# One tile a round by one-row DMAs of SyncE and ScalarE in place of a gather of GpSimd

## The reference, cut to what matters

```python
# layer 0: attention over the edges of each dst node
h = x @ W
e = leaky_relu((h @ att_src)[src] + (h @ att_dst)[dst], 0.2)     # self loops added
e = exp(e - segment_max(e, dst)[dst])
x = layernorm(x + tanh(segment_sum(h[src] * (e / denom[dst])[:, None], dst) + bias))
# layer 1: messages
h = gelu(x @ W_pre + b_pre)
x1 = x + segment_sum(h[src] * edge_attr, dst)
x = layernorm(x + x1 + gelu(gelu(x1 @ W1 + b1) @ W2 + b2))
```

## Time and profile before

| | |
|---|---|
| median of 3 runs | 3743.58 us |
| the profiled execution, its whole time | 3744.99 us |
| its span | 3743.2 us |
| GpSimd busy | 2782.9 us (74%), 2950 instructions |
| VectorE busy | 2422.9 us (65%) |
| TensorE busy | 2393.7 us (64%) |
| ScalarE busy | 1303.4 us (35%) |
| mean busy share of the 16 DMA engines | about two tenths in layer 0, four in layer 1 |

### The profile page before, as it was taken

How to read it: one execution, slowest core, us unless ns; L and a number is a source line. 1 busy time by engine, 2 the same in 40 slices (tenths; PEclk the granted TensorE clock), 3 DMA queues, 4 the chain that set the end, 5 groups by cost and what they waited for, 6 DMA issues and landing times.

```text
span 3743.2 us, 65890 instructions
## 1 busy us (share of the span) xinstructions
PE 2393.7 (64%) x16704; PEld 1950.4 (52%) x16705; DVE 2422.9 (65%) x6240; ACT 1303.4 (35%) x3893; POOL 2782.9 (74%) x2950
## 2 busy tenths in 40 slices
PE   5443344344344444444445899999888898999988
PEld 3333333333333333333334777777777777777776
DVE  7444444444566666665656777777777778888886
ACT  5433344444455555555553111111111221111222
POOL 7777777777777777777774777777777777777776
PEclk7555555555555555555556999999999999999998
DMA  5222222222222222222223444444444344444442
GB/s 100 43 41 42 42 44 42 44 42 43 42 43 43 43 44 44 43 43 45 43 43 92 90 93 94 90 95 95 95 94 95 91 95 92 95 95 99 92 95 70
DMA packets 336783, 254.19 MB, mean 68 GB/s; under 512 B 239277, under 2 KB 264370, under 8 KB 336539
## 3 DMA queue, kind: packets, MB, share of 16 engines
q0 software_dynamic: 94016, 146.16, 19.4%
q1 hardware_dynamic: 227905, 99.65, 11.4%
q10 hardware_dynamic: 14618, 6.14, 0.6%
HBM read 244.43 MB, written 7.25 MB: 67 GB/s over the span
## 4 chain that ended last, share of the span: by engine, by line
POOL 42%; issue 22%; PE 12%; DVE 9%; ACT 8%; ACTq 2%; DMA 2%; DVEq 2%; POOLq 0%; SPq 0%
POOL rows L714 42%; PE bank L1161 7%; ACT other L812 4%; PE bank L1148 2%; DVE other L1409 2%; DMA rows<-table,src_i 2%; DVE attr L1412 1%; PE bank L1067 1%; DVE attr L1442 1%; ACTq L803 1%; ACT L855 1%; DVE hot L1613 1%; ACT far_dst L808 0%; ACTq L840 0%; DVEq L425 0%
## 5 line engine op out<-in xcount | busy, mean ns | idle before, releaser
L714 POOL DMA_INDIRECT rows<-table,src_i x2850 | 2695.5, 946 | 912.7 <-issue 851.3
L1161 PE MATMUL bank<-node,hot 128*128 128x288 bf16 x9310 | 1228.8, 294 | 27.7 <-issue 14.7
L1161 PEld LDWEIGHTS bank<-node,hot 128*128 128x128 bf16 x9310 | 931.8, 101 | 282.8 <-issue 17.7
L1613 DVE TENSOR_SCALAR hot<-node,key 128x642 bf16<-128x642 int16 x1862 | 870.2, 538 | 120.1 <-PE bank L1161 64.5
L1063 PE MATMUL bank<-top_diag,ones 40*128 40x40 f32 (+1 forms) x392 | 132.2, 438 | 869.8 <-DVE top_diag L1395 864.7
L1067 PE MATMUL bank<-onehot,rows 128*97 128x72 f32 (+1 forms) x3048 | 543.9, 368 | 85.8 <-issue 85.3
L1063 PEld LDWEIGHTS bank<-top_diag,ones 40*128 40x128 f32 (+1 forms) x392 | 97.8, 309 | 931.7 <-DVE top_diag L1395 926.3
L1067 PEld LDWEIGHTS bank<-onehot,rows 128*97 128x97 f32 x3048 | 512.0, 282 | 118.1 <-issue 117.5
L968 ACT ACTIVATE pair<-dst_i 128x8 f32 (+1 forms) x196 | 35.2, 180 | 1186.2 <-DVE rows L1639 928.9
L812 ACT ACTIVATE other<-iota,far_dst 128x72 f32 (+1 forms) x1564 | 384.3, 328 | 23.1 <-ACT far_dst L808 0.9
L1148 PE MATMUL bank<-onehot,rows 128*96 128x40 f32 (+1 forms) x3128 | 308.1, 256 | 87.9 <-DVE rows L1644 46.3
(11 more groups left out here) (204 smaller groups left out, 1857.2 us busy)
## 6 DMA issues: line engine op xcount, KB each, us to landing
attr<-in_edge_attr_dram SPq DMA_DIRECT2D x190, 336.0 KB
rows<-table,src_i POOLq DMA_INDIRECT x2850
node<-in_src_dram SPq DMA_DIRECT2D x39, 320.0 KB
attr<-in_edge_attr_dram SPq DMA_DIRECT2D x190, 48.0 KB
table<-x SPq DMA_DIRECT2D x12, 196.0 KB
node<-table SPq DMA_DIRECT2D x8, 288.0 KB, 5.1
table<-rowt ACTq DMA_DIRECT2D x15, 144.0 KB
out_dram<-rowt ACTq DMA_DIRECT2D x15, 144.0 KB
```

Of the source, the lines that this page charges most:

```text
L714: pool.indirect_dma_start(to, None, table, bass.IndirectOffsetOnAxis(ap=at, axis=0)).then_inc(landed, 16)
L1161: last = pe.matmul(p_got[t], hot[:, c % HOTS, i, t * P:(t + 1) * P], tab[:, a, :, :].rearrange("p k d -> p (k d)"), start=a == 0, stop=a = ...
L1613: last = v.tensor_scalar(hot[:, c % HOTS, i, :].rearrange("p (r e) -> p r e", r=3), src16[:, :, 0:ROW3], key[:, a:a + 1], None, ALU.is_equal)
```

## The change

In every round but the first, the eighth gathered tile (in layer 1 the seventh) of the fifth group, slot 4, is no longer gathered. Its 128 rows are fetched one by one: 128 plain DMAs of one row each, whose source address comes from a register. In layer 0 SyncE issues 100 of them and ScalarE 28, in layer 1 SyncE 70 and ScalarE 58. They land in one buffer `single` [128 x 98]. In layer 0 ScalarE copies them from there into the slot and the score to PSUM (`given`); in layer 1 VectorE multiplies straight out of `single` (`multiplied_row`). `single` is refilled after it was read.

The addresses, row number times bytes of a row, are made at the start: two loads collect the src numbers of these tiles for all rounds (39 x 128 numbers each, 4 bytes apart from each other in DRAM), ScalarE scales them and stores them to `row_at` in DRAM. Each round both engines load their part of a line of `row_at`, and ten numbers at a time into registers.

Where the rows are issued: in layer 0 SyncE issues 60 once `single` was read (third group of the round before), then waits for the end of that round, loads dst and src as before, and issues 40. ScalarE issues 10 in the fifth group, 10 and 8 in the first two groups of the next round, each time between L839 and `given`. In layer 1 SyncE issues 14 after each attribute load from the fourth slot on, ScalarE 15, 15, 15 and 13 after the feeds in groups 1 to 4.

```diff
+AT_ONCE = 10
+BY_SYNC0, AHEAD0 = 100, 60
+BY_SYNC1 = 70
...
+        def rowed(it, u):
+            return u == SLOTS - 1 and not first(it) and it is not ROUNDS
+
+        def row_bytes(eng, reg, table, n):
+            at = eng.snap(reg, True, min_val=0, max_val=(N - 1) * n * 4)
+            return table.rearrange("n d -> (n d)").bitcast(BYTE)[bass.ds(at, n * 4)].rearrange("(a b) -> a b", a=1)
+
+        def fetch_rows(eng, name, numbers, regs_at, table, n, first_row, landed):
+            for a in range(*regs_at, AT_ONCE):
+                b = min(a + AT_ONCE, regs_at[1])
+                regs = [eng.alloc_register(f"{name}{k}") for k in range(a, b)]
+                eng.load(regs, numbers[0:1, a:b])
+                for k, reg in enumerate(regs, a):
+                    eng.dma_start(row_place(first_row + k, n), row_bytes(eng, reg, table, n)).then_inc(landed, 16)
...
+            last_group = src[0:ROUNDS * SLOTS * GE].rearrange("(r e) -> r e", r=ROUNDS)[:, (SLOTS - 1) * GE:SLOTS * GE]
+            sp.dma_start(made_at[:, 0:P].rearrange("r (p j) -> r p j", j=1),
+                         last_group[:, 0:P * (TILES - 1)].rearrange("r (p j) -> r p j", j=TILES - 1)[:, :, TILES - 2:TILES - 1],
+                         allow_slow_non_contiguous=True).then_inc(s_last, 16)
...
+            def rows_begun0(it, name):
+                sp.wait_ge(sync_at_in, SYNC_AT0 + 16 * it)
+                sp.sem_inc(sync_go, 1)
+                sp.wait_ge(single_free, SINGLE0 + it - 1)
+                sp.sem_inc(sync_go, 1)
+                fetch_rows(sp, f"row0_{name}_", sync_at, (0, AHEAD0), table0, D2, 0, sync_row)
...
                 round_of(dst_i, dst, it, 1 - k, e0.dst[0], 1)
                 if not first(it):
                     round_of(src_i, src, it, 1 - k, e0.src[0], 1)
+                    rows_ended0(it)
+                else:
+                    sp.wait_ge(a_st, 16 * CHUNKS)
+                    sp.wait_ge(act_at_in, 32)
+                row_numbers0(it + 1)
+                rows_begun0(it + 1, it)
...
             def load1(it, k):
                 for u in range(SLOTS):
                     load_attr(it * SLOTS + u, it, u)
+                    load_rows1(it, u)
...
-                    for j in range(TILES):
+                    for j in range(TILES - rowed(it, u)):
                         row_gather(place0(u, it)[:, j * D2:(j + 1) * D2], table0, src_i[:, k, u, j:j + 1], e0.rows[u])
...
-                    for j in range(TILES - booked(it, u)):
+                    for j in range(TILES - booked(it, u) - rowed(it, u)):
...
-                    act.wait_ge(e0.rows[u], gathered(g, it))
-                act.activation(p_src, rows0(u, it)[:, :, D1], ACT.Copy).then_inc(t0.given, 1)
+                    act.wait_ge(e0.rows[u], gathered(g, it, u))
+                t = TILES - rowed(it, u)
+                if rowed(it, u):
+                    act.wait_ge(sync_row, SYNC_ROW0 + 16 * BY_SYNC0 * it)
+                    act.wait_ge(act_row, ACT_ROW0 + 16 * (P - BY_SYNC0) * it)
+                    act.activation(rows0(u, it)[:, t, :], single[:, :], ACT.Copy)
+                    act.activation(p_src[:, t:TILES], single[:, D1:D2], ACT.Copy).then_inc(single_free, 1)
+                act.activation(p_src[:, 0:t], rows0(u, it)[:, 0:t, D1], ACT.Copy).then_inc(t0.given, 1)
...
                         act.activation(onehot_x[:, 0:TILES * w], further_score[:, 0:TILES * w], ACT.Exp).then_inc(tx.w, 1)
+                rows_along0(it, u)
                 if later(g, it, u, 2):
                     given(*later(g, it, u, 2), ws[2])
...
+                if rowed(it, SLOTS - 1):
+                    if u == 0:
+                        load_row_numbers1(it)
+                    if u < SLOTS - 1:
+                        fetch_rows1(it, u)
+
+            BY_ACT1 = (0, 15, 30, 45, P - BY_SYNC1)
...
+            def multiplied_row(it, u):
+                v.wait_ge(sync_row, SYNC_ROW1 + 16 * BY_SYNC1 * it)
+                v.wait_ge(act_row, ACT_ROW1 + 16 * (P - BY_SYNC1) * it)
+                at = slice((TILES - 2) * D, (TILES - 1) * D)
+                v.tensor_tensor(rows[:, u, at], single[:, 0:D], p_attr[:, at], ALU.mult).then_inc(single_free, 1)
```

More of the change, by code:

```diff
@@ L26 @@
 BF16 = mybir.dt.bfloat16
+BYTE = mybir.dt.uint8
 ALU = mybir.AluOpType
@@ L188, in gnn @@
         win_tab = sb("win_tab", [1, 3, GROUPS + 1], INT32)
+        single = sb("single", [P, D2])
+        sync_at = upto[:, 0:P].bitcast(INT32)
+        act_at = run[:, 0:P].bitcast(INT32)
+        made_at = rowt[0:ROUNDS, 0, 0:2 * P].bitcast(INT32)
         group_no = sb("group_no", [TG, 2], INT32)
@@ L330, in gnn @@
         e1_fed = sem("e1_fed")
+        sync_row, act_row, single_free = s_w0, s_dsts, s_tab0
+        sync_at_in, act_at_in = s_x[0], s_x[len(parts) - 1]
+        sync_go, act_go = s_line, s_begun
+        FETCH_ROUNDS = ROUNDS - 1
+        SYNC_ROW0, ACT_ROW0, SINGLE0, SYNC_AT0, ACT_AT0 = 16 * 3, 16 * 6, 1, 16, 32
+        SYNC_ROW1 = SYNC_ROW0 + 16 * BY_SYNC0 * FETCH_ROUNDS
+        ACT_ROW1 = ACT_ROW0 + 16 * (P - BY_SYNC0) * FETCH_ROUNDS
+        SINGLE1 = SINGLE0 + FETCH_ROUNDS
+        SYNC_AT1, ACT_AT1 = SYNC_AT0 + 16 * FETCH_ROUNDS, ACT_AT0 + 16 * FETCH_ROUNDS
         p_top, p_topb, p_newp = bank[0][0:WIN, 0:P], bank[1][:, 0:WIN], bank[1][:, P:P + WIN]
@@ L660, in load_table, with fetch_rows1, load_rows1 @@
                     sp.dma_start(h32[0:N - FULL * P, FULL, :], table1[FULL * P:N, :]).then_inc(landed, 16)
+            SHARE1 = -(-BY_SYNC1 // SLOTS)
+            PORTION1 = [(k * SHARE1, min((k + 1) * SHARE1, BY_SYNC1)) for k in range(SLOTS)]
+            AHEAD1 = 3
+            def fetch_rows1(it, portion, name):
+                if portion == 0:
+                    sp.wait_ge(sync_at_in, SYNC_AT1 + 16 * it)
+                    sp.sem_inc(sync_go, 1)
+                    sp.wait_ge(single_free, SINGLE1 + it - 1)
+                    sp.sem_inc(sync_go, 1)
+                fetch_rows(sp, f"row1_{name}_", sync_at, PORTION1[portion], table1, D, 0, sync_row)
+            def load_rows1(it, u):
+                if first(it):
+                    return
+                if u < AHEAD1 and not second(it):
+                    fetch_rows1(it - 1, SLOTS - AHEAD1 + u, it)
+                if u == AHEAD1 - 1:
+                    sp.dma_start(sync_at[:, 0:BY_SYNC1], row_at[bass.ds(it, 1), 0:BY_SYNC1]).then_inc(sync_at_in, 16)
+                if u >= AHEAD1:
+                    fetch_rows1(it, u - AHEAD1, it)
             def load1(it, k):
@@ L687, in _ @@
             rounds(sp, load1, alone=2)
+            for k in range(AHEAD1):
+                fetch_rows1(ROUNDS - 1, SLOTS - AHEAD1 + k, "last")
             sp.wait_ge(e1.free, LAST + 1)
@@ L823, in given, with load_row_numbers0, fetch_rows0, rows_along0 @@
                 else:
-                    act.wait_ge(e0.rows[u], gathered(g, it))
-                act.activation(p_src, rows0(u, it)[:, :, D1], ACT.Copy).then_inc(t0.given, 1)
+                    act.wait_ge(e0.rows[u], gathered(g, it, u))
[6 more added lines that the diff above has]
+                act.activation(p_src[:, 0:t], rows0(u, it)[:, 0:t, D1], ACT.Copy).then_inc(t0.given, 1)
+            def load_row_numbers0(it):
+                act.dma_start(act_at[:, 0:P - BY_SYNC0], row_at[bass.ds(it, 1), P + BY_SYNC0:2 * P]).then_inc(act_at_in, 16)
+            BY_ACT0 = (0, 10, 20, P - BY_SYNC0)
+            def fetch_rows0(it, part, name):
+                if part == 0:
+                    act.wait_ge(act_at_in, ACT_AT0 + 16 * it)
+                    act.sem_inc(act_go, 1)
+                    act.wait_ge(single_free, SINGLE0 + it - 1)
+                    act.sem_inc(act_go, 1)
+                fetch_rows(act, f"row0_{part}_{name}_", act_at, BY_ACT0[part:part + 2], table0, D2, BY_SYNC0, act_row)
+            def rows_along0(it, u):
+                if it is ROUNDS:
+                    return
+                if True:
+                    if u == SLOTS - 2 and it is not ROUNDS - 1:
+                        load_row_numbers0(it + 1)
+                    if u == SLOTS - 1 and it is not ROUNDS - 1:
+                        fetch_rows0(it + 1, 0, it)
+                    if u < 2 and not first(it):
+                        fetch_rows0(it, u + 1, it)
+                else:
+                    if u == SLOTS - 2 and it is not ROUNDS - 1:
+                        load_row_numbers0(it + 1)
+                    if u < 3 and not first(it):
+                        fetch_rows0(it, u, it)
             def sloped(g, it, u, w):
```

41 lines of the change are left out of this document (36 added, 5 removed).

## The result

The changed kernel takes 4615.19 us (median of 4 runs, 4614.89 to 4618.25) against 3743.53 us for the kernel before on the same chip (3743.04 to 3744.62): a ratio of 1.233, 95% interval 1.231 to 1.235. The profiled execution spans 4613.4 us. The direction was right, the size was not: 3970 us was forecast, 4300 us was the top of the range.

A forecast was written before the change was run, and what follows sets the result against it. Back-to-back gathers were taken as the bound, with ScalarE's serial cycle (layer 0) and VectorE (layer 1) close behind in wide stages; 3745 + 216 + 14 + 4 - 24 + 13 = 3968, say 3970 us, range 3830 to 4300.

The forecast's parts named there:

- What a one-row DMA costs its issuer: Row issue on SyncE and ScalarE: 0.40 us a row, between 0.33 and 0.70, with 0.03 for the register load.
- rival 3: Both layers: rows over 0.46 us make SyncE bound layer 0's narrow rounds; 4298 us at 0.50; chance 0.15 for 4250 or more.
- Layer 0, ScalarE: Rows lengthen its serial cycle: +216 us in wide stage (72 nodes, rounds 19 to 38), +14 in narrow (40 nodes).
- Layer 0, SyncE: SyncE's 100 rows and loads take 46 us, under a round's 48.7; costed at nothing, bound from 0.46 us a row.
- The start: Before layer 0's first group: two loads of single numbers, mostly covered by present waiting, cost 4 us, bounds 0 and 25.
- Layer 1: Rows reach the fifth group's multiply 2 us late: +13 us wide stage, -24 us narrow stage, -11 us together.
- The rule on issuing: Skill's rule for DMA issue: sequencer time is usually small, so ScalarE's rows weigh little; prediction objected that issue is paid per row.
- Rival 1: Both layers: ScalarE's rows fall in time it waits anyway, gathers stay the bound, 3650 us; chance 0.13.
- (1): Layer 0, wide stage: L825 no longer waits for gathered rows; GpSimd waits for L1067 some 10 us a round.
- (2): ScalarE between L839 and L820: gaps of 4 us in three groups of each round, filled with row DMAs.
- (3): Layer 0 rounds, by SyncE's src loads: near 60 us wide and 50 to 51 us narrow.
- (4): Layer 1 rounds: 42.4 us early and 44 to 45 us late, with VectorE waiting for `single`.

The follow-up runs named there:

- moved_b: Changed kernel with row DMAs in layer 0 only, ScalarE's ten rows moved behind the two score copies and ahead of the slope: 3999.9 us.
- act_none: Changed kernel without ScalarE's rows and its waits, SyncE issuing its 100 and 70 as before: 4252.3 us.
- l1_only: Changed kernel with row DMAs in layer 1 only, layer 0 gathering 40 tiles a round, addresses still collected at the start: 4189.5 us.
- fixed_rows: Changed kernel with constant row addresses and no load of registers, so wrong rows are fetched: 4070.3 us.
- the tile for nothing: Changed kernel with each row DMA replaced by a semaphore increment; no row DMAs or register loads left in the trace: 3728.3 us.
- alternate_both_b: Changed kernel with rows in both layers only every second round, all by SyncE, up to twenty registers a load: 3888.11 us, ratio 1.0385.

## Why the prediction was right or wrong

The direction, the reading of both layers' bounds and the mechanism of layer 0 held. The 645 us between 3970 and 4615 us are three terms: layer 0's wide stage 275 for 216, its narrow stage with the start 152 for 18, layer 1 443 for -11.

- **What a one-row DMA costs its issuer: the step that failed first.** The sum took 0.40 us, and 0.50 us was measured. The DMA itself was cheaper than the earlier trace rows said: 0.23 us, and 0.32 us (median) from one to the next. The load of ten registers was put at 0.3 us, "near that for one", and took 1.1 or 2.33 us by turns, 0.17 us a row for SyncE. The bound of 0.28 us a row had held it, but I chose the low end by the number of instructions. "A register load by the piece" was in rival 3 at a small chance, and it is what happened.
- **Layer 0, ScalarE.** Right in kind: the bursts lie on the cycle, as the timeline and moved_b show. Forecast 10.8 us a wide round, measured 14.1 us; rival 3's 13.6 us at 0.50 us a row is near.
- **Layer 0, SyncE.** Its bound of 0.46 us a row was worked out and was passed. The narrow rounds are 55.9 us, rival 3's 56 us, and act_none has the same in both stages. At 0.40 us this was costed at nothing: of the terms of layer 0 it is the one left out, some 110 us.
- **The start.** 4 us were forecast; the first reload of src comes 1.4 us later. The first narrow round is 30 us longer; 21 us of that are there in act_none too, with SyncE's rows alone, and l1_only, which has the start without the rows, has none of it.
- **Layer 1: the largest miss, and a step left out.** I asked only when the last row lands, and came to 2 us late. At 0.50 us rival 3 had 7.6 us late, and the trace has 287.2 us in 38 rounds, 7.6 us. That the two agree is partly luck: ScalarE's 58 rows take 34.9 us of the round with what stands among them, 0.60 us a row and not 0.50 (its loads of ten and five cost 0.22 us a row), and the feeds of these groups are late as well. And it gives +167 us, where 443 were measured. Missing was the other thing that waits behind a burst: the feed of the next group. Fifteen rows with their two loads (2.36 and about 1.4 us) are some 8 us, and the feed is wanted again within the 8.7 us of a group and is itself 1 us long. I had counted the feeds as work in front of the rows (0.9 us) and never the rows as work in front of the feeds, though the prediction made just that argument for layer 0. VectorE's 250 us for L1116 are this term (5 us before), and fixed_rows, with bursts of some 4.5 us, has 13 us of it. By VectorE's waits the rows are 161 us of the 443, this term 245, and the rest, the longer waits for TensorE among it, 37. No run takes the feeds' lateness away alone, so the split is read from the trace. Second, SyncE: 70 rows at 0.50, five pairs of attribute loads at 1.1 us and the numbers are 43 us of a round of 43.7 us, with one buffer that must be read before it is refilled. By itself it costs 302 us, and ScalarE's part by itself 391 us.
- **The rule on issuing.** The profile of the changed kernel shows where the sentence of the Trainium skill (page DMA: Bandwidth & Descriptors, section Issuing engines are not separate DMA queues) misleads, that the sequencer's time to initiate a DMA is "usually small relative to the DMA itself". An issue of 0.23 us is small beside the 1.1 us from the last issue to the multiply, but the 100 and 28, or 70 and 58, of a round stand one behind another on their engine: the row DMAs alone are 27% of the chain, 46% with the loads and the rest of both sequencers. By the Trainium skill, page Perfetto Trace Analysis, section on the HWDGE DMA instruction, the generator of descriptors is locked for one sequencer at a time. The prediction drew from it that rows would cost up to twice as much where both engines issue; act_none, with ScalarE silent, has narrow rounds of the same length (55.6 and 55.9 us), and the 0.332 and 0.330 us above are the same price, so no such effect is seen here.
- **Rival 1** was impossible at any price: the tile for nothing gains 15 us, not 95. The wide stages have 1.2 and 1.3 us a round behind the gathers, as the earlier trace rows said, and in layer 0 the instructions around the rows use that up and make the round 1.8 us longer.
- **What the profile after would show**: (1) came true in kind, with GpSimd waiting 16 us a wide round for TensorE's sums (301 us in 56 times, 1080 to 2295 us) where 10 were forecast; (2) came true, 4.98 us for the 4 us of a gap; (3) wide 64 for 60 us, narrow 56 for 50 to 51; (4) failed in its times, 54 and 56 us for 42.4 and 44 to 45, though VectorE does wait for `single`.

## What to carry to other kernels

When DMAs are moved to an engine that also computes, ask twice: when do they land, and which instruction is queued behind them; the second is more than half of layer 1's loss by VectorE's waits. An engine that waits most of the time isn't free if its short instructions lie on a serial cycle, and the same burst costs some 3 us less where the engine waits anyway (4.5 us of gaps in a group for 4.98 and 2.77). A row by hand is worth it only on a queue with room: in layer 0 alone, 128 rows on SyncE every second round gained 0.36%, 100 on SyncE and 28 on ScalarE every round lost 11%. Even that small gain is not had on every chip: beside a kernel before of 5272 us the same code lost 6.6%.

## What the runs showed of the hardware

The time of a load of several registers goes with pieces and with its address: 1.1 us for ten numbers from a multiple of 16 bytes, 2.33 us from elsewhere; 1.60 and 3.28 us for fifteen; 1.45 us for twenty. Loads of twenty, all from multiples of 16 bytes, brought a row to 0.07 us of load in layer 0 of alternate_both_b, where ten at once cost 0.17 us and five at once 0.24 us. A one-row DMA holds its queue for 0.23 us, less than the 0.30 to 0.39 us of the earlier trace rows, and with its address from a register the next starts 0.32 us after it; with a constant address it was 0.29 us. Two engines that issue such DMAs at the same time didn't slow each other: 0.332 us a row of SyncE beside ScalarE's and 0.330 us without them.
